# The ternary layer of an eight-layer kernel: its first product from three bf16 parts of the input, its tiles alternating with halves of the second product

## The reference

```python
def _L2_ffn_ref(x, W_fc, W_proj):        # W_fc (1024, 256), W_proj (256, 1024)
    W = _ternary_weight(W_fc, 64)        # each group of 64: -s, 0 or +s, s the bf16 mean of |w|
    h = jnp.square(jax.nn.relu(x @ W.T))           # 1024 hidden columns
    h = _rms_norm(h)                               # h * rsqrt(mean(h*h) + eps), per row
    return h @ _ternary_weight(W_proj, 64).T
x = _layernorm(x + _L2_ffn_ref(x, ...), axis=-1)
```

## Time and profile before

| what | us |
|---|---|
| median of 3 runs | 1789.03 (1788.66 to 1795.54) |
| the profiled execution, whole time | 1797.26 |
| its span | 1795.5 |
| PE busy | 1652.9 (92% of the span) |
| DVE busy | 1042.1 (58%) |
| ACT busy | 766.0 (43%) |
| POOL busy | 408.7 (23%) |
| the ternary layer, from its first matmul to the last matmul of its second product | 1055.7 to 1184.3 |

### The profile page before, as it was taken

How to read it: one execution, slowest core, us unless ns; L and a number is a source line. 1 busy time by engine, 2 the same in 40 slices (tenths; PEclk the granted TensorE clock), 3 DMA queues, 4 the chain that set the end, 5 groups by cost and what they waited for, 6 DMA issues and landing times.

```text
span 1795.5 us, 25372 instructions
## 1 busy us (share of the span) xinstructions
PE 1652.9 (92%) x9788; PEld 985.1 (55%) x9788; DVE 1042.1 (58%) x1863; ACT 766.0 (43%) x1757; POOL 408.7 (23%) x456
## 2 busy tenths in 40 slices
PE   7999879999999999699997888986999999979998
PEld 4666544433333335445564455764777777764556
DVE  4666577787787772343444863325777787942222
ACT  3421235666767776222111121115677767731110
POOL 2321000001100000220000037703555555630000
PEclk9998879999999999889998999988999999999999
DMA  5000220000000002010000030000000020000000
GB/s 173 2 7 15 57 72 2 1 2 1 1 2 1 1 1 99 1 49 0 1 0 15 1 117 1 1 0 6 7 1 7 1 80 1 1 1 0 12 12 24
DMA packets 28360, 34.95 MB, mean 19 GB/s; under 512 B 5713, under 2 KB 24722, under 8 KB 27730
## 3 DMA queue, kind: packets, MB, share of 16 engines
q1 hardware_dynamic: 28242, 33.35, 5.9%
HBM read 23.74 MB, written 2.10 MB: 14 GB/s over the span
## 4 chain that ended last, share of the span: by engine, by line
PE 80%; DVE 11%; POOL 3%; ACT 3%; issue 3%; DMA 0%; SPq 0%; POOLq 0%; DVEq 0%; ACTq 0%
PE PS L1155 8%; PE PS L1142 7%; PE PS L1114 6%; PE PS L1396 6%; PE PS L1402 6%; PE PS L2234 6%; PE PS L1417 5%; DVE arena L1320 3%; PE PS L2223 3%; PE PS L2201 3%; PE PS L1898 2%; PE PS L1881 2%; PE PS L339 2%; PE PS L2177 2%; PE PS L1191 2%
## 5 line engine op out<-in xcount | busy, mean ns | idle before, releaser
L1244 ACT ACTIVATE arena<-PS 128x512 f32<-128x512 f32 (+3 forms) x640 | 319.7, 534 | 176.0 <-PE PS L1142 77.7
L1320 DVE TENSOR_REDUCE arena<-PS 128x1 f32<-128x1024 f32 (+7 forms) x320 | 330.0, 1061 | 97.5 <-PE PS L1116 69.8
L1142 PE MATMUL PS<-arena 99*128 99x512 bf16 (+3 forms) x640 | 205.9, 353 | 1.4 <-ACT arena L1244 1.0
L1114 PE MATMUL PS<-arena 96*128 96x512 bf16 (+3 forms) x640 | 178.9, 358 | 18.3 <-DVE arena L1320 17.5
L190 POOL TENSOR_TENSOR rstd<-ve,mhalf 128x4 f32<-128x4 f32 x32 | 32.3, 1008 | 602.9 <-DVE ve L218 602.8
L185 ACT ACTIVATE XT<-PS 128x1024 f32<-128x1024 f32 x32 | 32.8, 1024 | 282.6 <-PE PS L178 282.6
L1155 PE MATMUL PS<-arena 128*32 128x512 f32 (+3 forms) x1280 | 150.5, 542 | 2.8 <-ACT arena L1250 1.7
L1142 PEld LDWEIGHTS PS<-arena 99*128 99x128 bf16 x640 | 60.7, 99 | 147.4 <-ACT arena L1244 115.9
L1396 PE MATMUL PS<-XT,arena 128*128 128x512 f32 x256 | 122.7, 602 | 5.7 <-DVE R L200 3.5
L2336 ACT ACTIVATE arena<-arena 128x128 f32<-128x128 f32 x256 | 122.7, 484 | 1.4 <-DVE arena L2513 1.4
L1402 PE MATMUL PS<-XT,arena 128*128 128x512 f32 x256 | 121.5, 597 | 0.0
(11 more groups left out here) (239 smaller groups left out, 2825.5 us busy)
## 6 DMA issues: line engine op xcount, KB each, us to landing
arena<-arena SPq DMA_DIRECT2D x55, 128.0 KB, 2.4
XT<-in_L_attn_xT SPq DMA_DIRECT2D x4, 512.0 KB, 7.7
X<-in_L_attn_x SPq DMA_DIRECT2D x4, 512.0 KB, 9.2
arena<-in_L_attn_out_w SPq DMA_DIRECT2D x1, 2048.0 KB, 7.2
out<-X SPq DMA_DIRECT2D x4, 512.0 KB, 2.9
arena<-in_dmask SPq DMA_DIRECT2D x1, 1024.0 KB, 5.6
arena<-in_L_ffn_W_up SPq DMA_DIRECT2D x1, 1024.0 KB, 5.5
arena<-in_L_ffn_W_gate SPq DMA_DIRECT2D x1, 1024.0 KB, 7.7
```

Of the source, the lines that this page charges most:

```text
L1114: last = pe.matmul(flat[:, o:o + w], q, a.KS[0:SROWS, CH * kc:CH * kc + w], start=True, stop=kc < c)
L1142: last = pe.matmul(PS[:, b, lo:CH], a.KS[0:rows, P * j:P * (j + 1)], a.QS[0:rows, G1 * g + r, CH * c + lo:CH * (c + 1)], start=True, stop= ...
L1244: act.activation(a.PB[:, n % 3, r, lo:CH], PS[:, 4 + x % 3, lo:CH], ACT.Exp, scale=D0 ** -0.5).then_inc(a.e2, 1)
L1320: dve.tensor_reduce(dst, src, AX.X, ALU.max, negate=True).then_inc(a.m1, 1)
```

## The change

The first product's weights are written as bf16 (VectorE's third step writes into the buffer `wb[0]` of signs; the two steps `- w` and `+ w` are left out for that matrix, so that there are 16 pieces rather than 20). Its input is split into three bf16 parts that add up to the float32 value: `x_high` is the cast of `XT` to bf16 on ScalarE, `x_residual` is `XT` minus it on VectorE, `x_middle` is the cast of that on ScalarE, and `x_low` is the rest, on VectorE. Each works on a whole chunk (128 x 1024). Of each chunk's four pieces most are issued in the layer before, behind its tails; the last ones (`x_low` of chunks 2 and 3, `x_residual` and `x_middle` of chunk 3) stand inside the ternary layer. A tile of the first product is now six bf16 matmuls.

On TensorE the tiles of `up(c+1)` alternate with halves (four matmuls) of the four output tiles of chunk c. The ones matmuls stand in the middle of the second product. The squares of `h` are made by ScalarE (`square`, one tile behind the relu), and GpSimd only adds (seven additions for a chunk). The mean and the power -1/2 of chunk c stand behind tile 5 of chunk c+1.

```diff
@@ l2_act, l2_dve: the layer before
             tail_act(k, act, NC * 5 + c - 2, c - 2)
+            act.wait_ge(k.xt_done, NC * 4 + c - 1)
+            if c >= 3:
+                x_middle(k, act, c - 3)
+            x_high(k, act, c - 2)
...
         tail_act(k, act, NC * 5 + c, c)
+        act.wait_ge(k.xt_done, NC * 4 + c + 1)
+        x_middle(k, act, c - 1)
+        x_high(k, act, c)
...
         tail_dve(k, dve, st, NC * 4 + c, c)
+        if c >= 2:
+            x_low(k, dve, c - 2)
+        if c >= 1:
+            x_residual(k, dve, c - 1)
@@ ternary_dve
-        last = dve.tensor_tensor(q, q, sign, ALU.mult)
+        last = dve.tensor_tensor(sign if m == 0 else q, q, sign, ALU.mult)
@@ the parts of x
+def x_high(k, act, c):
+    act.activation(a.XP[:, c, 0, :, :], k.XT[:, :, CH * c:CH * (c + 1)], ACT.Copy).then_inc(a.x_cast, 1)
+def x_middle(k, act, c):
+    act.wait_ge(a.x_res, c + 1)
+    act.activation(a.XP[:, c, 1, :, :], a.xr, ACT.Copy).then_inc(a.x_cast, 1)
+def x_residual(k, dve, c):
+    dve.wait_ge(a.x_cast, X_HIGH[c])
+    if c >= 1:
+        dve.wait_ge(a.x_low, c)
+    dve.tensor_tensor(a.xr, k.XT[:, :, CH * c:CH * (c + 1)], a.XP[:, c, 0, :, :], ALU.subtract).then_inc(a.x_res, 1)
+def x_low(k, dve, c):
+    dve.wait_ge(a.x_cast, X_MIDDLE[c])
+    dve.wait_ge(a.x_res, c + 1)
+    dve.tensor_tensor(a.XP[:, c, 2, :, :], a.xr, a.XP[:, c, 1, :, :], ALU.subtract).then_inc(a.x_low, 1)
@@ l2f_pe
-            for kt in range(KT):
-                last = pe.matmul(PS[:, n % 2, :], a.up[:, kt, P * it:P * (it + 1)], k.XT[:, kt, CH * c:CH * (c + 1)],
-                                 start=kt == 0, stop=kt == KT - 1)
+        for kt in range(KT):
+            for part in range(3):
+                last = pe.matmul(PS[:, n % 2, :], a.up[:, kt, P * it:P * (it + 1)], a.XP[:, c, part, kt, :],
+                                 start=(kt, part) == (0, 0), stop=(kt, part) == (KT - 1, 2))
...
+    for c in range(NC):
+        if c + 1 < NC:
+            up(c + 1, 0)
+            up(c + 1, 1)
+        pe.wait_ge(a.h_s, HT * (c + 1))
+        pe.wait_ge(k.r_done, NC * 5 + c)
+        for d in range(2 * TPC):
+            if d == TPC:
+                squares(c)
+            down(c, d // 2, d % 2)
+            if c + 1 < NC and d + 2 < HT:
+                up(c + 1, d + 2)
+        if c >= 1:
+            tail_pe(k, pe, NC * 6 + c - 1, c - 1)
@@ l2f_act: behind each relu
+            if it >= 1:
+                square(c, it - 1)
+        square(c, HT - 1)
+        if c == 0:
+            x_middle(k, act, NC - 1)
@@ l2f_pool
-                st.link(pool.tensor_tensor(a.sq, h, h, ALU.mult))
-                st.link(pool.tensor_tensor(acc, acc, a.sq, ALU.add))
+            pool.tensor_tensor(acc, acc, a.sq[:, it % 2, :], ALU.add).then_inc(a.add_s, 1)
+            if it == 5 and c >= 1:
+                root(c - 1)
@@ l2f_dve
     hidden(0)
+    x_low(k, dve, NC - 2)
+    x_residual(k, dve, NC - 1)
     for c in range(NC):
         if c + 1 < NC:
             hidden(c + 1)
+        if c == 0:
+            x_low(k, dve, NC - 1)
```

More of the change, by code:

```diff
@@ L1760, in l2f_alloc @@
     a.r = v(14 * n, [P, 2, CH])
-    a.sq = v(14 * n + 1024, [P, CH])
-    a.acc = v(14 * n + 1536, [P, 2, CH])
-    a.rs = v(14 * n + 2560, [P, NT])
+    a.sq = v(14 * n + 1024, [P, 2, CH])
+    a.acc = v(14 * n + 2048, [P, 2, CH])
+    a.rs = v(19000, [P, NT])
     a.g64 = v(14 * n + 2576, [P, P])
-    a.up = a.q[:, 0, :].rearrange("p (t e) -> p t e", t=KT)
+    a.up = a.wb[0].rearrange("p (t e) -> p t e", t=KT)
+    a.XP = v(0, [P, NC, 3, KT, CH], BF16)
+    a.xr = v(4 * n, [P, KT, CH])
     a.down = a.q[:, 1, :].rearrange("p (t e) -> p t e", t=HT)
@@ L1775, in l2f_alloc @@
     a.part = k.sem("l2f_part_s")
-    a.acc_s = k.sem("l2f_acc_s")
+    a.sq_s, a.add_s = k.sem("l2f_hidden_squared"), k.sem("l2f_squares_added")
     a.ssq = k.sem("l2f_ssq")
@@ L1779, in l2f_alloc @@
     a.rms = k.sem("l2f_rms")
+    a.x_cast, a.x_res, a.x_low = k.sem("l2f_x_cast"), k.sem("l2f_x_residual"), k.sem("l2f_x_low")
 HALF2 = KT * HID // 2
@@ L1784 @@
                (1, 0): (1, 0, 0), (1, 1): (1, 0, 1), (1, 6): (1, 1, 0), (1, 7): (1, 1, 1), (2, 0): (1, 2, 0), (2, 1): (1, 2, 1)}
+TERNARY_DVE = [(0, step, half) for step in range(3) for half in range(2)] + [(1, step, half) for step in range(5) for half in range(2)]
 def ternary_sp(k, sp, I):
@@ L1842, in ternary_dve @@
     p = HT * (c - 1) + it - 4
-    m, step, half = p // 10, p % 10 // 2, p % 2
-    if not 0 <= m < 2:
+    if not 0 <= p < len(TERNARY_DVE):
         return
+    m, step, half = TERNARY_DVE[p]
     cols = slice(HALF2 * half, HALF2 * (half + 1))
@@ L1867, in l2f_sp @@
     pass
+def x_high(k, act, c):
+    a = k.l2f
+    act.activation(a.XP[:, c, 0, :, :], k.XT[:, :, CH * c:CH * (c + 1)], ACT.Copy).then_inc(a.x_cast, 1)
+def x_middle(k, act, c):
+    a = k.l2f
+    act.wait_ge(a.x_res, c + 1)
+    act.activation(a.XP[:, c, 1, :, :], a.xr, ACT.Copy).then_inc(a.x_cast, 1)
+def x_residual(k, dve, c):
+    a = k.l2f
+    dve.wait_ge(a.x_cast, X_HIGH[c])
+    if c >= 1:
+        dve.wait_ge(a.x_low, c)
+    dve.tensor_tensor(a.xr, k.XT[:, :, CH * c:CH * (c + 1)], a.XP[:, c, 0, :, :], ALU.subtract).then_inc(a.x_res, 1)
@@ L1870, in l2f_pe @@
+def x_low(k, dve, c):
+    a = k.l2f
+    dve.wait_ge(a.x_cast, X_MIDDLE[c])
+    dve.wait_ge(a.x_res, c + 1)
+    dve.tensor_tensor(a.XP[:, c, 2, :, :], a.xr, a.XP[:, c, 1, :, :], ALU.subtract).then_inc(a.x_low, 1)
+X_HIGH, X_MIDDLE = (1, 3, 5, 7), (2, 4, 6, 8)
 def l2f_pe(k, pe):
     a, PS = k.l2f, k.PS
[L1872 to L1879, removed]
-            for kt in range(KT):
-                last = pe.matmul(PS[:, n % 2, :], a.up[:, kt, P * it:P * (it + 1)], k.XT[:, kt, CH * c:CH * (c + 1)],
-                                 start=kt == 0, stop=kt == KT - 1)
-            last.then_inc(a.mm, 1)
@@ L1885, in main, with up @@
[L1885 to L1890, removed]
+    pe.wait_ge(a.part, len(TERNARY_DVE))
+    def up(c, it):
+        n = HT * c + it
+        if it == 0:
+            pe.wait_ge(a.x_low, c + 1)
+        if n >= 2:
+            pe.wait_ge(a.r_s, n - 1)
+        for kt in range(KT):
+            for part in range(3):
+                last = pe.matmul(PS[:, n % 2, :], a.up[:, kt, P * it:P * (it + 1)], a.XP[:, c, part, kt, :],
+                                 start=(kt, part) == (0, 0), stop=(kt, part) == (KT - 1, 2))
+        last.then_inc(a.mm, 1)
@@ L1891, in main, with down, squares @@
+    def down(c, j, half):
+        for it in range(HT // 2 * half, HT // 2 * (half + 1)):
+            last = pe.matmul(f_tile(k, j), a.h[:, c % 2, it, P * j:P * (j + 1)], a.down[:, it, :],
+                             start=it == 0, stop=it == HT - 1)
+        if (j, half) == (TPC - 1, 1):
+            last.then_inc(k.f_ready, 1)
+    def squares(c):
+        pe.wait_ge(a.add_s, ADDS2 * (c + 1))
         if c >= 1:
@@ L1895, in main, with square @@
         last.then_inc(a.ssq, 1)
[L1896 to L1903, removed]
+    for it in range(HT):
+        up(0, it)
+    for c in range(NC):
[12 more added lines that the diff above has]
+            tail_pe(k, pe, NC * 6 + c - 1, c - 1)
+    tail_pe(k, pe, NC * 7 - 1, NC - 1)
+ADDS2 = HT - 1
 def l2f_act(k, act, st):
     a = k.l2f
+    def square(c, it):
+        n = HT * c + it
+        act.wait_ge(a.h_s, n + 1)
+        if it == 0:
+            if c >= 2:
+                act.wait_ge(a.ssq, c - 1)
+            dst = a.acc[:, c % 2, :]
+        else:
+            if it >= 3:
+                act.wait_ge(a.add_s, ADDS2 * c + it - 2)
+            elif c >= 1:
+                act.wait_ge(a.add_s, ADDS2 * c + 1 - it)
+            dst = a.sq[:, it % 2, :]
+        act.activation(dst, a.h[:, c % 2, it, :], ACT.Square).then_inc(a.sq_s, 1)
     for c in range(NC):
@@ L1924, in squares, with root @@
     def squares(c):
[L1925 to L1933, removed]
-                st.link(pool.tensor_tensor(a.sq, h, h, ALU.mult))
-                st.link(pool.tensor_tensor(acc, acc, a.sq, ALU.add))
-        pool.tensor_scalar(a.sq[:, 0:1], a.sq[:, 0:1], 1.0, 0.0, ALU.mult, ALU.add).then_inc(a.acc_s, 1)
-        pool.wait_ge(a.acc_s, c + 1)
+        acc = a.acc[:, c % 2, :]
+        for it in range(1, HT):
+            pool.wait_ge(a.sq_s, HT * c + it + 1)
+            if ADDS2 * c + it >= 2:
+                pool.wait_ge(a.add_s, ADDS2 * c + it - 1)
+            pool.tensor_tensor(acc, acc, a.sq[:, it % 2, :], ALU.add).then_inc(a.add_s, 1)
+            if it == 5 and c >= 1:
+                root(c - 1)
+    def root(c):
+        pool.wait_ge(a.ms, c + 1)
+        rs = a.rs[:, TPC * c:TPC * (c + 1)]
+        pool.tensor_tensor(rs, rs, k.mhalf[:, 0:TPC], ALU.pow).then_inc(a.rms, 1)
     squares(0)
@@ L1942, in l2f_pool @@
             squares(c + 1)
-        pool.wait_ge(a.ms, c + 1)
-        rs = a.rs[:, TPC * c:TPC * (c + 1)]
-        pool.tensor_tensor(rs, rs, k.mhalf[:, 0:TPC], ALU.pow).then_inc(a.rms, 1)
+        else:
+            root(c)
```

(17 more changed lines are left out.)

## The result

| | before | after |
|---|---|---|
| median, us | 1789.22 (1788.66 to 1795.54) | 1775.44 (1775.15 to 1777.59) |
| the profiled execution, whole time and span | 1797.26, 1795.5 | 1775.56, 1773.6 |

What follows compares the result with a forecast made beforehand. TensorE, busy for 92% of the span, was taken as the bound. Gains 14.1 + 9.5 = 23.6 less losses 1.75 + 3.0 + 1.6 = 6.35 net 17.2: 1789.03 - 17.2 = 1771.8 us, range 1764 to 1780.

Steps and rivals of the forecast that it cites:

- rival (a): Chunk 0: GpSimd's additions and VectorE's operations exclude each other, 1.96 us a tile, 2.5 us lost, 1774.3 us; chance 0.14.
- The forecast for the profiled execution alone: Whole profiled execution: 1797.26 us before, less the net gain of 17.2, leaves 1780.1 us.
- The bf16 tiles: First product on TensorE: six bf16 matmuls, 1.29 us a tile instead of 1.73, gain 14.1 us over 32 tiles.
- The order and the squares: TensorE's waits in the ternary layer: gap of 6.54, low clock 2.0 and one wait of 0.95 go, gain 9.5 us.
- the two reasons given for the end of the gap: Gap of 6.54 us ahead of chunk 2: GpSimd has seven operations, not fifteen; the power leaves its place behind all squares.
- The parts in the layer before: VectorE's subtractions behind the tails of chunks 1 and 2 start the ternary layer 1.75 us later (0.3 to 3.0).
- The parts inside the layer: Chunk 1's first relu waits behind x_middle(3): TensorE stands 3.0 us (2.0 to 4.0), plus 1.6 for the clock.
- The clock term of 1.6: TensorE's lower clock after the new wait at chunk 1's first relu: 1.6 us lost (0 to 2.0).
- (b): Ternary layer: the chain through x_middle(3) is short or hidden and the clock stays, 1767.2 us; chance 0.10.
- (c): First product on TensorE: bf16 weight loads do not hide, costing 19.2 us, 1791.0 us; chance 0.04.
- (d): First product: tiles no faster, waiting for ScalarE; half the gain lost to edges and handovers gives 1779 us; chance 0.08.
- walk through in time: Ternary layer: the last second product ends at about 1167.3 us instead of 1184.4, agreeing with the net 17.2.

Runs made afterwards that it cites:

- the float32 tiles: The changed kernel with float32 first-product weights and tiles from XT, without the parts of x; 1783.9 us, ratio to the kernel before 0.9954.
- the kernel once more: The changed kernel run again with nothing altered, as yardstick for the other runs; 1777.4 us, ratio to the kernel before 0.9922.
- the additions short: The changed kernel with GpSimd's additions of chunk 0 on one column instead of 512, leaving out that chunk's sum of squares; 1767.2 us.
- the late cast: The changed kernel with ScalarE's cast x_middle(3) moved from ahead of chunk 1's first relu to behind its fifth; 1769.7 us, then 1767.8.

## Why the prediction was right

The median lies in the range, 3.6 us above the forecast and 1.1 from the 1774.3 of rival (a); the gain by the stretches is 15.5 us of 17.2. The mechanism was right, and one term was too small. Term by term the runs give 13.4 + 10.1 - 1.55 - 0.4 - 6.4 = 15.2 us. That the tiles gave 0.7 less and the order 0.6 more cancels by luck. The forecast for the profiled execution alone, 1780.1, was 4.5 us too high; it could not know of the 4.9 us ahead of the change.

- **The bf16 tiles (14.1).** Spacing 0.215 and tile 1.29 as forecast, an edge between bf16 and float32 costs nothing (a step is 3.02 = 1.29 + 1.73). A step with a float32 tile is 3.44, so it is 0.42 x 32 = 13.4. The runs give 12.7 and 12.1; the gap of 0.74 that ends chunk 0 is in these, and is counted below.
- **The order and the squares (9.5).** 10.1 by the float32 tiles. But of the two reasons given for the end of the gap the first was not needed: fewer operations on GpSimd, as the kernel with its squares there shows. Whether the place of the power would have been enough without the new order on TensorE, no run shows.
- **The parts in the layer before (1.75).** 1.55, the same two subtractions, in front of the same sum. The first relu was expected to cost nothing, as TensorE would be at 0.50 of its clock for 5.3 us. In the trace of after the clock read 0.50 for only 3.0 us, the two tiles were done sooner, and TensorE waited 0.39 us for the relu. In the kernel once more the clock stayed low longer and there was no such gap.
- **The parts inside the layer (3.0 and 1.6 for the clock).** The right chain and the right place, too small. TensorE's gaps are 0.74 + 3.99 = 4.7 us and the clock cost 1.7, together 6.4 instead of 4.6. This term is the main miss: I put 1.0 us on the chain for GpSimd's additions, and they cost 1.06 + 0.88 on the two subtractions alone and brought the last squares of chunk 0 to one in 1.68 us. The clock term of 1.6 was met in one trace and passed in the other (1.7 and 2.9).
- **Rival (a)** was thus more than a rival. With the additions short, the extra is gone. Its pace of 1.96 us a tile was too high (1.68), and its 2.5 us stand against 6.4 - 4.6 = 1.8. The Trainium skill (SBUF — State Buffer, "SBUF: two separate sides") has an exclusive lock between these operations, for the whole instruction. The traces agree in kind, with VectorE's 1.22 going to 2.28 us and GpSimd's 1.01 to 1.92, each ending about 1 us after the other. They do not agree in size: a square and an addition that excluded each other for their whole recorded times of 0.69 and 1.27 us could not come every 1.68.
- **Rivals (b), (c), (d)** did not happen: the chain was not short, the weight loads (99 ns) are hidden, the tiles did not wait in later chunks.

A slip in the prediction's walk through in time: the last second product ended at 1184.3 before, not at 1184.4; nothing hangs on it. That the medians show 13.8 and the stretches 15.5 I leave open; the interval of 11 to 18 us covers both.

## What to carry to other kernels

A cast or copy for a later chunk must not stand in an engine's queue ahead of the operation that frees a buffer for TensorE: moving one cast by five tiles gave 6 us. Before work is moved off an engine to end a wait, look at the place of the awaited operation in that engine's queue; here, with the place and the order changed, moving the work gave nothing more. And a wait of VectorE for a small GpSimd operation was no free slot for a two-input VectorE operation: the power took 1.92 us instead of 1.01.

## What was not expected of the hardware

A gap of 2.68 us in TensorE at the same place of the layer before lowered the clock in four of eleven executions and left it up in seven. The first matmuls behind it in the kernel with squares on GpSimd, and in the kernel with the late cast:

```profile
997.58 2.42 PE L1636 MATMUL PS<-XT,arena 128*64 128x512 f32 x4 [2.68 <-DVE R L200]
```

```profile
996.89 1.93 PE L1636 MATMUL PS<-XT,arena 128*64 128x512 f32 x4 [2.68 <-DVE R L200]
```

A gap of 3.99 us cost 1.7 us of clock in one execution and 2.9 in another of the same kernel. In the kernel without alternation one gap of 3.08 us left the clock up and one of 2.22 us was followed by a low one. The clock's cost behind a gap of 2 to 4 us is thus a range and no number.
